# A gather kernel for graph messages: its add of gathered rows made in two operations, with the landing counts split evenly

## The reference

```python
ef  = relu(edge_attr @ We1 + be1) @ We2 + be2          # edge_attr: 106250 x 64
ef  = ef * sigmoid(timestamps[:, None] @ Wt + bt)
combined = concatenate([x[row], ef], axis=1)           # x[row]: the source node of each edge
msg = relu(combined @ Wn1 + bn1) @ Wn2 + bn2
out = segment_sum(msg, col, num_segments=6250) + x     # col: the destination node
y   = layernorm(x + out)
```

## Time and profile before

| | |
|---|---|
| median of three runs | 1438.06 us |
| the profiled execution: its time, and its span | 1437.05 us, 1435.3 us |
| PE busy | 966.9 us, 67% |
| POOL busy | 783.2 us, 55% |
| DVE busy | 649.6 us, 45% |
| ACT busy | 580.0 us, 40% |

### The profile page before, as it was taken

One profiled execution on the slowest core, in us unless ns is written; L12 is line 12 of the kernel. 1 busy time (PEld: TensorE's weight loads), 2 busy tenths in 40 slices (PEclk: granted clock), 3 DMA queues, 4 the chain that ended last, 5 costly groups with the idle time before them and its releaser, 6 DMA issues.

```text
span 1435.3 us, 18308 instructions
## 1 busy us (share of the span) xinstructions
PE 966.9 (67%) x5031; PEld 722.8 (50%) x5032; DVE 649.6 (45%) x1688; ACT 580.0 (40%) x656; POOL 783.2 (55%) x834
## 2 busy tenths in 40 slices
PE   3638767676677767666767667676766766765765
PEld 3626544554555545444545455555444545553454
DVE  1425533444445445344444444444543635544446
ACT  1316433443444425443444344443443534442442
POOL 7270456555655555556555565556555555655640
PEclk7768888798898889888878788889988977887978
DMA  6433332333423323333233233333332423333310
GB/s 183 142 110 110 103 114 89 95 114 93 131 83 108 114 88 115 106 100 124 85 91 121 92 101 113 100 121 89 105 114 85 136 86 112 112 102 112 96 30 18
DMA packets 72025, 148.62 MB, mean 104 GB/s; under 512 B 18295, under 2 KB 47030, under 8 KB 65254
## 3 DMA queue, kind: packets, MB, share of 16 engines
q1 hardware_dynamic: 42918, 89.72, 18.4%
q0 software_dynamic: 26400, 54.12, 14.3%
q10 hardware_dynamic: 2592, 3.48, 0.7%
HBM read 140.85 MB, written 6.40 MB: 103 GB/s over the span
## 4 chain that ended last, share of the span: by engine, by line
another core or an unknown queue 42%; ACT 21%; PE 19%; issue 11%; DVE 5%; ACTq 2%; DVEq 0%
ACT tw L663 9%; PE psS L820 6%; PE psM L862 5%; ACT h L596 4%; PE psH L875 4%; PE psE L887 2%; ACT h L671 2%; ACT eaT L630 1%; ACT found L593 1%; ACT x_sb L684 1%; DVE efw L1162 1%; DVE onehot L1147 1%; ACT staged_own L699 1%; DVE h L1141 1%
## 5 line engine op out<-in xcount | busy, mean ns | idle before, releaser
L536 POOL DMA_INDIRECT gathered<-node_table,src_e x793 | 751.6, 948 | 594.6 <-DVE h L1141 328.5
L820 PE MATMUL psS<-onehot,h 128*128 128x128 f32 x1656 | 294.1, 350 | 259.5 <-ACT h L596 234.2
L820 PEld LDWEIGHTS psS<-onehot,h 128*128 128x128 f32 x1656 | 274.2, 258 | 278.3 <-ACT h L596 140.7
L671 ACT ACTIVATE h<-psH,be_c 128x1024 f32<-128x1024 f32 x104 | 115.9, 1115 | 666.4 <-remote 522.0
L1141 DVE TENSOR_TENSOR h<-psM,gathered 128x1024 f32<-128x1024 f32 (+1 forms) x104 | 122.8, 1183 | 552.2 <-remote 503.4
L862 PE MATMUL psM<-wn,efw 128*128 128x128 f32 x1664 | 233.7, 298 | 31.6 <-issue 25.5
L862 PEld LDWEIGHTS psM<-wn,efw 128*128 128x128 f32 x1664 | 226.8, 217 | 29.1 <-issue 21.6
L663 ACT ACTIVATE tw<-ew,bt_c,wt_c 128x1024 f32<-128x1024 f32 x104 | 234.2, 2253 | 4.8 <-DVE efw L1162 3.5
L887 PE MATMUL psE<-h,we 128*128 128x512 f32 x416 | 217.4, 644 | 5.5 <-issue 5.4
L1162 DVE SCALAR_TENSOR_TENSOR efw<-psE,be_c,tw 128x1024 f32<-128x1024 f32 x104 | 133.0, 1279 | 94.4 <-remote 45.3
L1147 DVE TENSOR_SCALAR onehot<-split_ids,dst_e 128x65 f32<-128x65 f32 x832 | 173.8, 271 | 0.3
(11 more groups left out here) (112 smaller groups left out, 363.1 us busy)
## 6 DMA issues: line engine op xcount, KB each, us to landing
ew<-in_edge_weight SPq DMA_DIRECT2D x52, 1024.0 KB
ea<-in_edge_attr SPq DMA_DIRECT2D x52, 512.0 KB
row_tiles<-node_table SPq DMA_DIRECT2D x896, 0.5 KB
gathered<-node_table,src_e POOLq DMA_INDIRECT x793
x_sb<-in_x SPq DMA_DIRECT2D x6, 512.0 KB, 6.3
out_y<-x_sb ACTq DMA_DIRECT2D x12, 256.0 KB
node_table<-gathered SPq DMA_DIRECT2D x7, 256.0 KB, 2.1
node_table<-h SPq DMA_DIRECT2D x4, 256.0 KB
```

Of the source, the lines that this page charges most:

```text
L536: pool.indirect_dma_start(to, None, rows, bass.IndirectOffsetOnAxis(index, 0)).then_inc(landed, 16)
L671: nc.scalar.activation(h1[:, s % 2, :], psH[:, :, :].rearrange("p r e -> p (r e)"), ACT.Relu, bias=be1_c[:, :]).then_inc(h1_ready, 1)
L820: return nc.tensor.matmul(to, h[:, (k - SUM_LAG) % BODY * PAIR + q, t * C:(t + 1) * C], hot, start=(t == 0), stop=(t == TILES - 1))
```

## The change

`PART` becomes four and four: the first group's four landings count on the first semaphore, the second group's on the second. `pre` makes two adds of 512 elements instead of one of 1024, one for each group. The first waits for the product and for the first semaphore, the second also for the second semaphore (at place 0 for the row tile that ACT moves, too); the second alone raises `pre_ready`. PE's wait ahead of its first layer is now met by four landings, not by six. The pairs that don't gather (0 to 3) keep one add.

```diff
-PART = (6, PAIR * TILES - 6)
+PART = (TILES, TILES)
...
             def pre(g, i, k):
                 place = (k - MSG_LAG) % BODY
-                at = slice(place * PAIR, (place + 1) * PAIR)
                 dve.wait_ge(msg_ps, g + 1)
                 if isinstance(g, int) and g < RAW // PAIR:
-                    rows = raw_pairs[g]
+                    at, rows = slice(place * PAIR, (place + 1) * PAIR), raw_pairs[g]
...
+                    make_pre(h[:, at, :], psM[:, :, :], rows).then_inc(pre_ready, 1)
                 else:
-                    rows = gathered[:, at, :]
                     turn = i - 1 if k < MSG_LAG else i
                     dve.wait_ge(gather_in[place][0], turn * (16 * PART[0]))
+                    make_pre(h[:, place * PAIR, :], psM[:, 0, :], gathered[:, place * PAIR, :])
                     if place == 0:
                         dve.wait_ge(gather_in[place][1], gathered_by(turn) * 16)
                         wait(dve, rows_moved, row_tiles_by(turn))
                     else:
                         dve.wait_ge(gather_in[place][1], turn * (16 * PART[1]))
-                make_pre(h[:, at, :], psM[:, :, :], rows).then_inc(pre_ready, 1)
+                    make_pre(h[:, place * PAIR + 1, :], psM[:, 1, :], gathered[:, place * PAIR + 1, :])\
+                        .then_inc(pre_ready, 1)
```

## The result

The changed kernel takes 1445.85 us (median of 8 runs, 1439.69 to 1449.46), the kernel before, run beside it, 1436.99 us (8 runs, 1434.12 to 1442.18). The ratio is 1.0054, with a 95% interval of 1.0032 to 1.0076: 0.54% slower, 7.8 us, with 4.6 to 10.9 us inside the interval. (The medians differ by 8.9 us; a difference in us is worked out here from the ratio and the median of the kernel before, except where two medians are given with it.) Measured again on another chip, in ten runs, it was 1.0039 (1.0016 to 1.0062), 5.6 us. The forecast was +4.7 us and slower. The profiled execution of the changed kernel has a span of 1443.9 us.

What follows compares the result with a forecast made beforehand. The prediction took a loop of POOL's gathers, PE's late signals and DVE's add as the bound. Counts 0, plus 4.1 and 0.6 us for the add, gave +4.7 on 1438.06: 1442.8 us, range 1440 to 1446.

Steps and rivals of the forecast that it cites:

- What bounds the kernel: A 13.47 us loop per pair: POOL's gathers 9.70, PE's signals seen 1.77 later, add 1.23, next gather 0.77.
- The landing counts and PE's wait, 0: Waits of PE and the first add are met before they are reached, with six or four landings: 0 us.
- The add in two, +0.053 us a pair: DVE's two adds of 681 ns, overlapping by 85, take 1277 ns instead of 1224: +0.053 us a pair.
- Rival (a): DVE's two half adds don't overlap: 12 to 16 us more, 1450 to 1454 us; chance 0.12.
- the 158 ns: Extra cost per pair of two DVE adds by the skill's formula, 2 x 691 - 1224; 15.6 us over 99 pairs.
- Who sees it, 77 and half of 22: POOL's 77 waits for the add pay in full, 4.1 us; the other 22 pairs count half, 0.6 us.
- The number: Forecast time of the whole changed kernel: 1442.8 us, +4.7 us, own range 1440 to 1446; chance 0.46.
- (b): Rival: the second add's extra time is hidden by PE's signal timing or back-to-back bursts; 1438 us; chance 0.17.
- (c): Rival: number of POOL bursts run on end changes, 1.9 us each; four more 1435 (chance 0.13), fewer 1450 (0.08).
- (d): Rival: the "remote" idle is the landing of gathers; 43 us saved, 1395 us; chance 0.04.
- The sign that I had given for (d): The "remote" idle of DVE's add L1141 falling by tens of us would show that gather landings cause it.

Runs made afterwards that it cites:

- e5: Kernel before, with the second group's four gathers left out from pair 8 to 102 (sums wrong): 1035.7 us beside 1437.9, ratio 0.721.
- e7: Kernel before, with POOL stopping between a pair's first and last four gathers until PE has given its product: 1348.1 us beside 1437.9, ratio 0.938.
- e12: Changed kernel with two more DVE operations (128 and 256 elements, written to unread tiles) ahead of the first add: ratio 1.0269 to the kernel before.
- e2: Kernel before with only the landing counts changed to four and four, one add of 1024 kept: ratio 0.9992.
- e3: Kernel before without PE's wait for landings ahead of its first layer: ratio 0.9982.
- e1: Kernel before with only the add cut in two, landing counts left at six and two: ratio 1.0029, 4.2 us slower.
- the two long doses: Changed kernel with its add in four operations of 256 (1.0068), and with two extra unneeded operations ahead of the add (1.0269), both against the kernel before.

## Why the prediction was right

*What bounds the kernel.* Shown. The loop of POOL's burst, PE's late signals and the add is what most of the time is made of: shorten the burst (e5) and 402 us go, take the add out of it (e7) and 89 us go, lengthen the way through the add (e12) and 38.6 us come.

*The landing counts and PE's wait, 0.* Right: e2 and e3 are both within 0.2% or so of no change, and both intervals hold 1.

*The add in two, +0.053 us a pair.* Right: 2 x 685 ns, and the timeline has 1.29 us from start to end where one add had 1.23; from the add's start to POOL's next gather it is 2.05 us for 2.00, and on one chip the median turn is 0.06 us longer with two adds (e1, e2). The overlap of some 0.08 us stands behind a met wait as it did for L1162. Rival (a), no overlap, fell by this row, and with it the 158 ns that the prediction had worked out from the Trainium skill (VectorE: DVE Perf Modes, The DRAIN you can't avoid). The prediction left out a sentence of that section: "A next op that is not held starts earlier". That is what the records here show: a boundary costs 0.06 us, not 0.16.

*Who sees it, 77 and half of 22.* The weak step. The 22 was misread: two bursts run on end 13 times, POOL waits 83 times (seven of these under "issue"), and three adds have no gathers behind them. And I counted each wait in full, while the two long doses pay for 54 and 64 pairs, not 88. By the greater, the change's 0.06 us would be 3.8 us; the change measured 7.8 and 5.6, with intervals that begin at 4.6 and 2.3, and its adds alone 4.2. The forecast of 4.7 lies inside all three intervals; whether the true cost is 4 or 7 us they don't tell.

*The number.* The mechanism was right, and the size is right as far as these measurements reach. That 1445.85 us fell inside 1440 to 1446 is in part luck: it is 0.15 us from the upper end, and the change cost 1.7 times what was forecast in the one measurement, 1.2 times in the other.

*Rivals.* (b), hidden, fell: both measurements of the change lie above 1 beyond their intervals. (c), another pattern of bursts: the number on end does vary, 12 to 18 in the profiles with one or two adds, but not so that it could make the loss: in e1 and e2 it is 12 with two adds and with one. (d), landings, fell for PE by e3, and for DVE by e7: POOL's own wait for PE's product, which no landing meets, ends just as late (the add starts at 738.38, POOL goes on 0.74 us later). The sign that I had given for (d), a "remote" idle that falls by tens of us, did come, 33 us, and was a bad one: on one chip the sum was 567.5 us with one add (e2) and 557.5 with two (e1).

## What to carry to other kernels

Read a wait of one engine on another as a loop before pricing an operation by its engine's busy share: DVE was 45% busy, and yet some 0.6 us of every added microsecond came out at the end. Cutting an operation in two pays only if somebody is waiting for the first part; the same cut with a release in it turned 0.4% lost into 1.3% gained. And where an engine stands behind a chain of two (a signal, then an operation on it), let it wait for the earlier one if the data allow it: three lines did far more than the change.

## What the runs showed of the hardware

PE's signals came about 1.8 us after POOL's run of indirect gathers had ended: 1.77 us in the kernel before, the median over the 64 adds that wait for "remote" right behind a burst, and 1.74 to 1.85 in the twelve other profiles with eight gathers a pair (e5's is the exception). PE's own records had ended long before. In the step of the earlier trace rows the last product ends at 765.51 and the add starts 5.85 us later:

```profile
763.56 1.95 PE L862 MATMUL psM<-wn,efw 128*128 128x128 f32 x16
```

With four gathers on end the "remote" idle went from 503.4 to 16.6 us, and the add at 508.25 started 1.18 us after the end of its product. Whether POOL's writing of descriptors, the transfers themselves or something else holds the signals back, no run here separates.
